# One group of eight token tiles in place of two groups of four in the output projection

## What is computed

```python
xn = (x - mean(x)) / sqrt(var(x) + 1e-5)
# attention
q = (xn @ Wq).reshape(b, s, 32, 128);  k, v = split(xn @ Wkv)      # one kv head of 128
scores = einsum('bqhd,bkd->bhqk', q, k) * scale + alibi_bias       # causal
attn_out = einsum('bhqk,bkd->bqhd', softmax(scores), v).reshape(b, s, h) @ Wo
# experts: rank 8 each, top 16 of 64
gate = softmax over the top 16 of (xn @ Wq_w.T) @ keys.T, zero elsewhere
z = (xn @ A_w.T) * gate                                            # 512 columns
ffn_out = (z @ B_w.T) * 2
out = x + attn_out + ffn_out
```

## Time and profile before

| | us |
|---|---|
| median of 3 runs | 5736.2 |
| lowest and highest run | 5724.9, 5859.7 |
| the profiled execution | 5720.8 |
| its span on the slowest core (core 1) | 5719.2 |
| spans of the eight cores | 5704.5 to 5719.2 |
| mean granted clock of TensorE, all cores | 0.80 |
| the output projection of the first chunk, from its first matmul to the first instruction of the next chunk | 775.3 |
| the same of the second chunk, to the end | 763.2 |

### The profile page before, as it was taken

One profiled execution on the slowest core, in us unless ns is written; L12 is line 12 of the kernel. 1 busy time (PEld: TensorE's weight loads), 2 busy tenths in 40 slices (PEclk: granted clock), 3 DMA queues, 4 the chain that ended last, 5 costly groups with the idle time before them and its releaser, 6 DMA issues.

```text
span 5719.2 us, 42946 instructions; the slowest of 8 cores (5704.5 to 5719.2 us)
## 1 busy us (share of the span) xinstructions
PE 3662.3 (64%) x15108; PEld 1490.0 (26%) x15108; DVE 1288.6 (23%) x2247; ACT 1185.7 (21%) x1884; POOL 223.4 (4%) x239
## 2 busy tenths in 40 slices
PE   1676666665665677775476666666676777567777
PEld 1332222221111233322232222333221221123333
DVE  4211121234444000002311112222333333200000
ACT  4002232222212000001202223334333333200000
POOL 0000000000000000000000000000000000000000
PEclk9887777777777888887687777777888888888888
DMA  5353222211110777776343122112011010387776
GB/s 120 56 70 54 40 49 46 45 28 15 15 15 0 122 135 138 137 136 135 89 59 60 40 44 46 31 31 38 6 15 15 0 15 0 61 139 138 133 140 126
DMA packets 355052, 369.22 MB, mean 65 GB/s; under 512 B 29216, under 2 KB 315936, under 8 KB 348960
## 3 DMA queue, kind: packets, MB, share of 16 engines
q0 software_dynamic: 311360, 232.37, 29.6%
q1 hardware_dynamic: 25056, 100.54, 5.3%
q10 hardware_dynamic: 18432, 33.56, 1.5%
HBM read 563.74 MB, written 33.55 MB: 104 GB/s over the span
## 4 chain that ended last, share of the span: by engine, by line
PE 51%; DMA 19%; DVE 14%; ACT 9%; issue 6%; DVEq 0%; ACTq 0%; POOL 0%; POOLq 0%; SPq 0%
PE ps_a L437 19%; PE ps_a L835 7%; PE ps_c L835 6%; DMA astream<-wo 6%; DMA out<-scratch 5%; DVE scratch L608 4%; DMA wstream<-wq 4%; PE ps_c L557 3%; ACT astream L756 3%; PE ps_t L562 3%; PE ps_s L575 3%; DMA scratch<-x 2%; ACT astream L594 2%; PE ps_c L700 2%; DVE scratch L746 2%
## 5 line engine op out<-in xcount | busy, mean ns | idle before, releaser
L437 PE MATMUL ps_a<-xnT,wstream 128*128 128x512 bf16 x4096 | 1108.5, 438 | 103.2 <-DMA wstream<-wq 103.0
L835 PE MATMUL ps_a<-astream,QC 128*128 128x512 bf16 x2048 | 665.1, 409 | 445.5 <-DVE scratch L871 293.4
L835 PE MATMUL ps_c<-astream,QC 128*128 128x512 bf16 x2048 | 657.0, 404 | 0.0
L594 ACT ACTIVATE astream<-ps_s,scratch 128x512 bf16<-128x512 f32 x628 | 425.0, 687 | 1052.5 <-PE ps_s L575 776.4
L437 PEld LDWEIGHTS ps_a<-xnT,wstream 128*128 128x128 bf16 x4096 | 449.5, 111 | 738.4 <-issue 395.8
L700 PE MATMUL ps_c<-scratch,vT 128*128 128x256 bf16 x735 | 208.3, 383 | 497.4 <-DVE scratch L675 197.2
L756 ACT ACTIVATE astream<-scratch,cols 128x128 bf16<-128x128 f32 (+10 forms) x240 | 207.2, 863 | 1220.2 <-DVE scratch L746 1218.5
L557 PE MATMUL ps_c<-astream,vT 128*128 128x512 bf16 x680 | 283.8, 417 | 197.0 <-ACT astream L594 187.1
L835 PEld LDWEIGHTS ps_a<-astream,QC 128*128 128x128 bf16 x2048 | 205.2, 103 | 740.6 <-issue 544.7
L448 DVE TENSOR_SCALAR QC<-ps_a 128x512 bf16<-128x512 f32 x128 | 88.5, 692 | 1266.7 <-PE ps_a L437 1089.5
L871 DVE TENSOR_TENSOR scratch<-ps_a,scratch 128x512 f32<-128x512 f32 x64 | 43.9, 690 | 1191.9 <-PE ps_a L863 1189.2
(11 more groups left out here) (90 smaller groups left out, 2405.5 us busy)
## 6 DMA issues: line engine op xcount, KB each, us to landing
astream<-wo POOLq DMA_DIRECT2D x128, 1024.0 KB, 10.3
wstream<-wq POOLq DMA_DIRECT2D x64, 1024.0 KB, 14.5
scratch<-x SPq DMA_DIRECT2D x16, 2048.0 KB, 8.6
scratch<-x SPq DMA_DIRECT2D x128, 256.0 KB, 5.5
out<-scratch ACTq DMA_DIRECT2D x128, 256.0 KB, 6.0
scratch<-ab SPq DMA_DIRECT2D x30, 1088.0 KB, 5.1
astream<-awt POOLq DMA_DIRECT2D x16, 1024.0 KB, 10.8
wstream<-bwt POOLq DMA_DIRECT2D x16, 512.0 KB, 12.6
```

The lines of the kernel that those rows point to most:

```text
L437: E.matmul(ps_a[b][:], wq_half_view[hh][:, kk % 16, mm * 128:(mm + 1) * 128], xnT[:, kk, t2 * 512:(t2 + 1) * 512], start=(kk == 0), stop=( ...
L594: ii=idx: E.activation(astream[:, ss * 1024:ss * 1024 + 512], b[:, 0:512], AF.Exp, bias=v_bc[:, hh, ii:ii + 1]), inc="ac")
L835: k8_=k8, ss=sl2, tt=t: E.matmul(b[:], QC[:, kk, tt * 128:(tt + 1) * 128], wo_slab[ss][:, k8_, :], start=(kk == 0), stop=False),
```

## The change

The loop over `tg` is taken away. The list of banks is extended to all eight, and each slab of `wo` is used for all eight token tiles before the next is taken. The final matmuls, adds and stores run over eight tiles in a row. The order of issue within the group is otherwise the same: the x of the first two tiles is loaded after the third quarter, and that of every further tile when the tile two before it has been added. The two buffers each for slabs, x and results are unchanged.

```diff
         fbanks = [("ps_a", 0, ps_a[0]), ("ps_a", 1, ps_a[1]),
-                  ("ps_c", 0, ps_c[0]), ("ps_c", 1, ps_c[1])]
+                  ("ps_c", 0, ps_c[0]), ("ps_c", 1, ps_c[1]),
+                  ("ps_s", 0, ps_s[0]), ("ps_s", 1, ps_s[1]),
+                  ("ps_t", 0, ps_tf[0]), ("ps_t", 1, ps_tf[1])]
         for fsp in range(8):
...
-            for tg in range(2):
-                for ti in range(4):
-                    p.need("tensor", fbanks[ti][:2])
-                for quarter in range(4):
+            for t in range(NT):
+                p.need("tensor", fbanks[t][:2])
+            for quarter in range(4):
...
-                        for ti in range(4):
-                            t = tg * 4 + ti
-                            pe_q = p.op("tensor", lambda E, b=fbanks[ti][2], kk=k,
+                    for t in range(NT):
+                        pe_q = p.op("tensor", lambda E, b=fbanks[t][2], kk=k,
...
-                            inc="pe" if (k8 == 7 and ti == 3) else None)
-                    p.release(("astream", sl2), "pe", pe_q)
-                    if quarter == 2:
-                        for ti in (0, 1):
-                            t = tg * 4 + ti
-                            sl = t % 2
+                            inc="pe" if (k8 == 7 and t == NT - 1) else None)
+                p.release(("astream", sl2), "pe", pe_q)
+                if quarter == 2:
+                    for t in (0, 1):
+                        sl = t % 2
...
-                for ti in range(4):
-                    t = tg * 4 + ti
-                    sl = t % 2
-                    if ti >= 2:
+            p.wait("tensor", "dgw%d" % par, g_b)
+            for t in range(NT):
+                sl = t % 2
+                if t >= 2:
...
+                p.release(fbanks[t][:2], "dv", dv_o)
+                p.release(("xrd", sl), "dv", dv_o)
+                p.wait("scalar", "dv", dv_o)
```

More of the change, by code:

```diff
@@ new lines, in build_program @@
+            for t in range(NT):
+                p.need("tensor", fbanks[t][:2])
+            for quarter in range(4):
+                sl2 = quarter % 2
+                p.need("gpsimd", ("astream", sl2))
+                g_wo = p.op("gpsimd", lambda E, qq=quarter, ss=sl2, ff=fsp:
+                            E.dma_start(
+                    out=wo_slab[ss],
+                    in_=dwo.rearrange("(q p) n -> p q n", p=128)
+                        [:, qq * 8:(qq + 1) * 8, ff * 512:(ff + 1) * 512]),
+                    inc="dgo%d" % sl2, incby=16)
+                p.wait("tensor", "dgo%d" % sl2, g_wo)
+                pe_q = None
+                for k8 in range(8):
+                    k = quarter * 8 + k8
+                    for t in range(NT):
+                        pe_q = p.op("tensor", lambda E, b=fbanks[t][2], kk=k,
+                                    k8_=k8, ss=sl2, tt=t: E.matmul(
+                            b[:], QC[:, kk, tt * 128:(tt + 1) * 128],
+                            wo_slab[ss][:, k8_, :],
+                            start=(kk == 0), stop=False),
+                            inc="pe" if (k8 == 7 and t == NT - 1) else None)
[3 more added lines that the diff above has]
+                        sl = t % 2
@@ L855, in build_program @@
                         p.need("sync", ("xrd", sl))
-                        xrd_ds[t] = p.op("sync", lambda E, r=tok0 + t * 128, ss=sl,
-                                         ff=fsp: E.dma_start(
+                        xrd_ds[t] = p.op("sync", lambda E, r=tok0 + t * 128,
+                                         ss=sl, ff=fsp: E.dma_start(
                             out=v_xrd[ss], in_=dx[r:r + 128, ff * 512:(ff + 1) * 512]),
                             inc="dsr%d" % sl, incby=16)
-                    pe_f = None
@@ L861, in build_program @@
[L861 to L879, removed]
@@ L880, in build_program @@
-                    p.release(("ost", sl), "do%d" % sl, do_v)
+            p.wait("tensor", "dgw%d" % par, g_b)
+            for t in range(NT):
+                sl = t % 2
+                if t >= 2:
+                    p.need("sync", ("xrd", sl))
+                    xrd_ds[t] = p.op("sync", lambda E, r=tok0 + t * 128, ss=sl,
+                                     ff=fsp: E.dma_start(
+                        out=v_xrd[ss], in_=dx[r:r + 128, ff * 512:(ff + 1) * 512]),
+                        inc="dsr%d" % sl, incby=16)
+                pe_f = None
+                for n in range(4):
+                    pe_f = p.op("tensor", lambda E, b=fbanks[t][2], nn=n, pp=par,
+                                tt=t: E.matmul(
+                        b[:], zgT[:, nn, tt * 128:(tt + 1) * 128], b_view[pp][:, nn, :],
+                        start=False, stop=(nn == 3)),
+                        inc="pe" if n == 3 else None)
+                pe_fin_last = pe_f
+                p.wait("vector", "pe", pe_f)
+                p.wait("vector", "dsr%d" % sl, xrd_ds[t])
+                p.need("vector", ("ost", sl))
+                dv_o = p.op("vector", lambda E, b=fbanks[t][2], ss=sl: E.tensor_add(
+                    v_ost[ss], b[:], v_xrd[ss]), inc="dv")
+                p.release(fbanks[t][:2], "dv", dv_o)
+                p.release(("xrd", sl), "dv", dv_o)
+                p.wait("scalar", "dv", dv_o)
+                do_v = p.op("scalar", lambda E, r=tok0 + t * 128, ss=sl, ff=fsp:
+                            E.dma_start(
+                    out=dout[r:r + 128, ff * 512:(ff + 1) * 512], in_=v_ost[ss]),
+                    inc="do%d" % sl, incby=16)
+                p.release(("ost", sl), "do%d" % sl, do_v)
```

22 lines of the change are left out of this document (removed).

## The result

| | before | after |
|---|---|---|
| median of the runs, us | 5796.4 (10 runs) | 5494.4 (9 runs) |
| lowest run | 5724.9 | 5487.6 |
| profiled execution | 5720.8 | 5490.6 |
| its span on the slowest core | 5719.2 | 5489.0 |

The ratio of the times is 0.954, with a 95% interval from 0.949 to 0.959. The two profiled executions differ by 230.2 us, and the forecast was 230.

The account below looks back on a forecast made before the run. PE stands still over a quarter of the output projection, waiting for the bank-emptying adds and wo loads. Savings of 187 us inside panels, 34 between them and 8 at the ends make 230: 5720.8 - 230 = 5491 us, range 5425 to 5590.

Parts of the forecast that it names:

- A quarter against a slab: Output projection, inside a panel: doubled quarters of 13.8 us hide the wo loads; 57.7 us a panel, 187 us saved.
- The emptying of the banks: Between panels: one chain of adds through two buffers each; restart 24.4 us after the first L863 matmul, 34 us saved.
- The ends: Last panel of each chunk's output projection: shorter ends, 24 us in the first and 19.4 in the second, 8 us saved.
- A: Rival, gaps between panels: tiles 4 to 7 pay contended rounds of 8.8 us; +92, 5583 us; chance 10%.
- B: Rival, inside panels: the waits for wo stay, with slabs of 14 us; +62, 5553 us; chance 6%.
- C: Rival, gaps between panels: first round shorter too, rounds an uncontended 4.5 us; -60, 5431 us; chance 17%.
- D: Rival, dense matmul stretches: granted clock falls to the lower level beyond the first 31 us; 5987 us, slower; chance 3%.
- The limiter: Rival, dense matmuls: the skill's peak-current limit at 13/16 clock eats the whole gain, 230 us; 5721 us; chance 3%.
- The rule of the Trainium skill on rotating banks: Between groups: rotate independent groups through banks so emptying overlaps matmuls; taken to lose nothing here, sum left as it is.

Follow-up runs that it names:

- the densest kernel: The changed kernel with eight in-place buffers for x and result, and TensorE asking for the banks one by one: 5208.0 us, ratio 0.908 to the kernel before.

## Why the prediction was right

It was right in its time (5491 forecast, 5490.6 in the profiled execution, 5494.4 the median) and in its mechanism, step by step. That the two times agree to less than 1 us is luck: the ends of the stages were 4 us longer than forecast, the 14 gaps together 3 us shorter, and the eight cores of this one execution are 17 us apart.

- **A quarter against a slab.** The waits for wo inside a panel were costed at nothing; none is left. The work time of a panel was forecast at 57.7 us, and is 57.7 in the mean of 16: 256 steps and 12 matmuls at the lower level, where 11 were taken. The run with doubled reads shows the mechanism: with the traffic of before, a quarter of 13.8 us still never waits. The run with halved slabs bears it out in the old form: there a shorter load goes under the short quarter, and the waits go.
- **The emptying of the banks.** Forecast adds at F+10.4, 12.5, 15.8, 17.9, 21.2, 23.4, measured in the mean 10.7, 12.7, 15.6, 18.1, 20.7, 23.2; forecast restart F+24.4, measured 24.2. The decision that carried this was to give tiles 4 to 7 the price of transfers with no slab beside them, from the earlier trace rows. The runs with doubled reads and with deeper buffers confirm both sides of it: with slabs beside them the second round costs twice as much, and without the buffers' chain the gap is 8.1 us. The slab was also the right reason for the long first round: that round takes 9.4 us in the mean, and 4.9 in the last panel of the kernel, where no slab is beside it.
- **The ends.** Both were taken about 2 us too short. The kernel ends 20.9 us after the last F, not 19.4, and L214 starts at F+26.5, not F+24. In the first chunk's last panel the eighth add came only at F+20.5, in the second's at F+17.9; the load of the next chunk's x runs beside the last stores in the first alone. The second stage was forecast at 651.8 us and took 652.8, the first at 656.4 and took 657.0.
- **The rivals.** A was right in its total and wrong in its condition: a gap of 31 us was forecast for contended rounds and 31.5 measured, but it takes the traffic of before to bring it about, and then the rounds are 10.8 and 6.0 us, not 8.8 twice, so the total agrees in part by chance. B fell with the waits. C had the first round wrong: tile 2 stayed at F+10.7, since the second slab is issued after F in both kernels. D fell with whole panels at a clock of 1.00 after the cold start, and with 480 us of matmuls at 1.00 in the densest kernel. The limiter did not show in the profiled execution of the change or of the densest kernel, so it did not eat the gain; but a level of 0.81 does occur, as the row of the doubled-reads run shows. The forecast's sentence that the trace doesn't bear it out was true of one trace and too weak a ground for 3%: three of the twelve kernels profiled here have that level on some cores. The rule of the Trainium skill on rotating banks (Perfetto Trace Analysis, Optimizing Tensor Performance, Matmuls) was dismissed as changing nothing in the sum, and that holds for this change. As advice for the old form it was good, since rotating the banks brought that form 3.5%; the wait then moved to the slabs.

What the forecast didn't see is how much the stage still had to give. It took the chain through two buffers as given and priced it, and the chain was 14 x 16.1 = 225 us of what was left. The kernel with eight in-place buffers and the banks asked for one by one takes 5208 us, 9% less than before and 5% less than the change.

## What to carry to other kernels

Where an engine waits at a boundary, count how often the boundary comes and how many rounds through the buffers it holds: making groups twice as large halved the first and tripled the second, and the gain came mostly from elsewhere, the loads that a doubled quarter could hide. Price a DMA by what runs beside it in that stretch, not by its median, and when you free a buffer, look at which queue uses it next and when, since an early prefetch can take back what it was to give.

## What the runs showed of the hardware

- The same store of 256 KB lands in 2.0 us with nothing beside it (x loads held back), in 4.4 us in the median beside an x load of the same size, in 6.2 to 8.7 us beside a slab with the x loads held back, and in 7.8 to 10.3 us beside a slab and x loads. An x load takes 4.1 to 4.3 us in the median. Whether the transfers get in each other's way in the DMA engines or at HBM, no run here tells apart.
- The clock of TensorE stayed at its upper level, 2.4 GHz, for 480 us of 128x128 by 128x512 matmuls, with no pause over 1 us, on all eight cores, at a step of 0.216 us. Yet in three other profiled executions (rotated banks, doubled reads, halved slabs) some cores were granted 0.81 for stretches, up to 82 us long, with a step of 0.262 us. It came to neighbouring pairs of cores at the same times and to others not at all. The Trainium skill (TensorE: Matmul & The Clock Gate, Part 1) tells of a limiter at 13/16, which is 0.8125, the level that these rows show, and of its coming once three cores of a die run dense matmuls. The second half doesn't hold here, since the densest kernel ran without it and the less dense one with rotated banks had it on the same chip. What brings it on stays open. The cores that have it for 249 us or more took up to 93 us longer than the others of the same execution, and for that the comparisons above were read from single cores.
- After 1.05 us of idle time TensorE restarted at the upper level; after 16 us its first 10 to 14 matmuls of a panel ran at the lower one.
